# Work behind the value products done once per pair of tasks, one projection per slot

## The reference

```python
q, k, v = x @ wq + bq, x @ wk + bk, x @ wv + bv        # per head
x = layernorm(x + softmax(q k^T / sqrt(8)) v @ wo.T + bo)
# cross attention: per-head weights Wk, Wq, Wv (8 x 8); queries from x, keys and values from the context
x = layernorm(x + softmax((x Wq) (ctx Wk)^T / sqrt(8)) (ctx Wv) @ Wo.T)
# feed-forward 128 -> 512 -> 128, with activations and weights quantised to 8 bits over the whole tensor
x = layernorm(x + qlinear(gelu(qlinear(x, W1, b1)), W2, b2))
```

## Time and profile before

| | |
|---|---|
| median of 3 runs | 370.28 us (369.21 to 370.56) |
| profiled execution | 369.99 us, its span 368.3 us |
| attention stage | 25 to 285 us of the span |
| busy, whole span | DVE 329.0 us (89%), PE 269.9 (73%), ACT 254.9 (69%), POOL 189.1 (51%) |
| L771, maxima | 128 times, 155.7 us |
| L608 and L619, exponentials | 128 times, 131.2 us |
| TensorE's clock | 1.0 of full speed from 84 to 222 us |

### The profile page before, as it was taken

How to read it: one execution, slowest core, us unless ns; L and a number is a source line. 1 busy time by engine, 2 the same in 40 slices (tenths; PEclk the granted TensorE clock), 3 DMA queues, 4 the chain that set the end, 5 groups by cost and what they waited for, 6 DMA issues and landing times.

```text
span 368.3 us, 13210 instructions
## 1 busy us (share of the span) xinstructions
PE 269.9 (73%) x4899; PEld 172.1 (47%) x4899; DVE 329.0 (89%) x715; ACT 254.9 (69%) x501; POOL 189.1 (51%) x382
## 2 busy tenths in 40 slices
PE   3668778998898988989889898888882557102970
PEld 2445545565665655656556565555541312001640
DVE  5658798899999999999999999999989499998994
ACT  2136867787888877878788787777761499505965
POOL 5245778566656656566565566756122005400385
PEclk9999999899999999999999999999996565655796
DMA  1352332323323233232332323322000000000024
GB/s 50 100 152 68 85 88 61 97 74 105 96 76 104 83 89 103 70 105 69 103 104 70 110 73 105 91 83 76 10 5 1 0 0 0 0 0 3 0 87 142
DMA packets 48998, 25.19 MB, mean 68 GB/s; under 512 B 6440, under 2 KB 48808, under 8 KB 48936
## 3 DMA queue, kind: packets, MB, share of 16 engines
q1 hardware_dynamic: 48216, 24.02, 22.7%
q10 hardware_dynamic: 720, 0.33, 0.3%
HBM read 9.39 MB, written 2.10 MB: 31 GB/s over the span
## 4 chain that ended last, share of the span: by engine, by line
DVE 38%; PE 18%; issue 16%; POOL 10%; SPq 9%; ACT 4%; DMA 3%; DVEq 0%; POOLq 0%; ACTq 0%
DVE neg_max L771 14%; SPq L348 6%; DVE h_ext L880 5%; DVE h_ext L881 5%; PE ps L995 4%; PE ps L1021 4%; PE ps L1037 3%; POOL rstd L486 2%; DVE arena_q L905 2%; ACT probs L619 2%; POOL o_root L553 2%; DMA arena_h<-parts_cq 2%; DVE r_sum L781 2%; PE ps L1074 1%; PE ps L1063 1%
## 5 line engine op out<-in xcount | busy, mean ns | idle before, releaser
L771 DVE TENSOR_REDUCE neg_max<-ps 128x8 f32<-128x1024 f32 x128 | 155.7, 1216 | 12.4 <-PE ps L995 10.8
L608 ACT ACTIVATE probs<-ps 128x1024 f32<-128x1024 f32 x64 | 65.6, 1025 | 19.9 <-PE ps L1002 18.7
L995 PE MATMUL ps<-arena_h 31*128 31x128 f16 x1024 | 53.0, 222 | 34.7 <-DVE neg_max L771 22.7
L619 ACT ACTIVATE probs<-ps 128x1024 f32<-128x1024 f32 x64 | 65.6, 1025 | 17.2 <-PE ps L1002 15.8
L995 PEld LDWEIGHTS ps<-arena_h 31*128 31x128 f16 x1024 | 31.0, 95 | 67.5 <-DVE neg_max L771 41.9
L483 POOL TENSOR_TENSOR var_eps<-mean_var,eps_col 128x1 f32<-128x1 f32 x64 | 12.2, 191 | 82.0 <-DVE mean_var L818 82.0
L1002 PE MATMUL ps<-arena_h 32*128 32x128 f16 x1024 | 51.8, 219 | 0.5 <-ACT probs L608 0.5
L1021 PE MATMUL ps<-probs,arena_q 128*32 128x128 f32 x1024 | 42.2, 284 | 0.9 <-issue 0.9
L1021 PE MATMUL ps<-probs,arena_h 128*32 128x128 f32 x1024 | 41.2, 279 | 0.2 <-ACT probs L608 0.2
L486 POOL TENSOR_TENSOR rstd<-var_eps,minus_half 128x1 f32<-128x1 f32 x64 | 35.2, 550 | 5.2 <-PE ps L1021 0.2
L1002 PEld LDWEIGHTS ps<-arena_h 32*128 32x128 f16 x1024 | 29.6, 93 | 1.6 <-issue 0.9
(11 more groups left out here) (152 smaller groups left out, 642.5 us busy)
## 6 DMA issues: line engine op xcount, KB each, us to landing
arena_h<-parts_sq SPq DMA_DIRECT2D x48, 64.0 KB, 2.0
arena_h<-parts_ck SPq DMA_DIRECT2D x48, 64.0 KB, 2.0
arena_h<-parts_cq SPq DMA_DIRECT2D x48, 64.0 KB, 2.1
arena_h<-parts_sk SPq DMA_DIRECT2D x45, 64.0 KB, 2.0
xT_in<-in_xT_dram SPq DMA_DIRECT2D x16, 128.0 KB, 2.4
xN_in<-in_xN_dram SPq DMA_DIRECT2D x16, 128.0 KB, 2.3
cT_in<-in_cT_dram SPq DMA_DIRECT2D x16, 128.0 KB, 2.5
cN_in<-in_cN_dram SPq DMA_DIRECT2D x16, 128.0 KB, 2.5
```

The costliest lines, as they stand in the source:

```text
L608: act.activation(probs[1][:, :], ps_s2, ACT.Exp, scale=SCALE).then_inc(ex, 1)
L619: act.activation(probs[0][:, :], ps_s2, ACT.Exp, scale=SCALE).then_inc(ex, 1)
L771: dve.tensor_reduce(neg_max[b.par][:, HH * half:HH * half + HH], ps_s1.rearrange("p (h k) -> p h k", h=HH), AXX, ALU.max, negate=True).the ...
L995: ins = pe.matmul(ps_s1[:, at:at + S], q[r:r + MAX_AT, j, :], kk[r:r + MAX_AT, j, :], start=True, stop=True, skip_group_check=True)
```

## The change

Everything behind the value products is done once for both tasks of a pair. `whole(k)` gives the pair only when k is its second task. `ps_u` holds four quarters instead of two, `u_sb` 512 columns, `r_sum`, `att`, `attT` both tasks. ScalarE copies `u` and `cq_full` in even slots and `attT` in odd ones; VectorE has reciprocal, aggregates and `att` in the odd slot's first gap, both norms behind its second maximum, `y_sb` (one instruction for self pairs, two for cross pairs) in the even slot's first gap and both statistics in its second. GpSimd does `var_eps` and `rstd` on two columns, in odd slots. Only one projection stands in a slot: q six ahead, k five, v four, context key five, always behind the second burst; the copies of q and v are in the next slot. The first five pairs keep q and k in one slot. Loads of xT move one slot earlier.

```diff
-QK_AT, V_AT, CK_AT, FILL_AT, VC_AT, BIAS_AT = 5, 4, 5, 4, 3, -1
-XT_AT, XN_AT, CT_AT, CN_AT = 7, 3, 8, 6
+Q_AT, K_AT, V_AT, CK_AT, FILL_AT, VC_AT, BIAS_AT = 6, 5, 4, 5, 4, 3, -1
+XT_AT, XT_LEAD_AT, XN_AT, CT_AT, CN_AT = 8, 7, 3, 8, 6
-LEAD_SLOTS = 2
+def whole(k):
+    t = task(k)
+    return t if t is not None and t.half == 1 else None
...
# gpsimd
-                v = task(k - 4)
+                v = whole(k - 4)
                 if v is not None:
-                    pool.wait_ge(ag, v.pos + 1)
-                    pool.tensor_tensor(var_eps[v.par][:, :], mean_var[v.par][:, 1:2], eps_col[:, :], ALU.add).then_inc(ve, 1)
+                    pool.wait_ge(ag, 2 * v.at + 2)
+                    pool.tensor_tensor(var_eps[v.lane][:, :], mean_var[v.lane][:, :, 1],
+                                       eps_col[:, 0:1].broadcast_to([128, 2]), ALU.add).then_inc(ve, 1)
...
# scalar
+                zz, w, v = whole(k - 1), whole(k - 2), whole(k - 5)
...
+                if v is not None and v.kind == "S":
+                    act.wait_ge(tx, v.pair + 1)
+                    need(act, split_done["cq"], v.pair - RING + 1)
+                    act.copy(cq_full[v.ring][:, :], ps_x[:, 0:PAIR]).then_inc(txe, 1)
+                if zz is not None:
+                    act.wait_ge(pv, 2 * zz.pos + 2)
+                    need(act, tu, zz.at)
+                    act.copy(u_sb[:, :], ps_u).then_inc(ue, 1)
...
# vector
-                b, w, x, v = task(k + 2), task(k - 2), task(k - 3), task(k - 4)
+                b = task(k + 2)
+                w, x, v = whole(k - 2), whole(k - 3), whole(k - 4)
...
# tensor
+                w, x, v = whole(k - 2), whole(k - 3), whole(k - 5)
...
-                        need(pe, ue, z.pos)
+                        need(pe, ue, z.at)
...
-                if k >= LEAD_SLOTS:
-                    projections()
                 scores(1)
...
                 product(1)
...
+                projections()
```

More of the change, by code:

```diff
@@ L85, in __init__ @@
         self.par = pos % 2
+        self.at = pos // 2
+        self.lane = self.at % 2
     @property
@@ L187, in decoder_layer @@
         probs = [sb(f"probs{i}", [128, HH * S]) for i in range(HALVES)]
[L188 to L194, removed]
+        u_sb = sb("u_sb", [128, 4 * S])
+        r_sum, att, attT = sb("r_sum", [128, 2 * H]), sb("att", [128, 2 * H, E]), sb("attT", [128, PAIR])
+        y_sb = [sb(f"y_sb{i}", [128, 2, D]) for i in range(2)]
+        stats = sb("stats", [128, 2, 6])
+        mean_var = [sb(f"mean_var{i}", [128, 2, 2]) for i in range(2)]
+        var_eps = [sb(f"var_eps{i}", [128, 2]) for i in range(2)]
+        rstd = [sb(f"rstd{i}", [128, 2]) for i in range(2)]
         x2_all = sb("x2_all", [128, B, D])
@@ L638, in slot @@
                                        scale=w_inv[:, j:j + 1]).then_inc(w_magic, 1)
-                if v is not None and v.kind == "S":
-                    act.wait_ge(tx, v.m + 1)
-                    need(act, split_done["cq"], v.pair - RING + 1)
-                    act.copy(cq_full[v.ring][:, v.half * S:v.half * S + S], ps_x[:, 2 * S:3 * S]).then_inc(txe, 1)
             over_slots(slot)
@@ L788, in slot @@
[L788 to L794 removed]
+                    for i in range(2):
+                        dve.wait_ge(bs, 2 * v.at + i + 1)
+                        dve.bn_aggr(mean_var[v.lane][:, i, :], stats[:, i, :]).then_inc(ag, 1)
@@ L1082, in slot @@
-                if k < LEAD_SLOTS:
-                    projections()
+                if v is not None and v.kind == "S":
+                    pe.wait_ge(xn, v.pos + 1)
+                    need(pe, tae, pairs_to(k - 3))
+                    need(pe, mte, min(max(k + 2, 0), TASKS))
+                    for i in range(2):
+                        last = pe.transpose(ps_x[:, i * S:(i + 1) * S], x1_all[:, v.m - 1 + i, :], ident[:, :])
+                    last.then_inc(tx, 1)
+                product(1)
@@ new lines, in slot @@
+                if w is not None:
+                    pe.wait_ge(an, w.at + 1)
+                    need(pe, mte, min(max(k + 2, 0), TASKS))
+                    need(pe, tae, w.at)
+                    need(pe, txe, s_pairs_to(k - 6))
+                    for i in range(2):
+                        last = pe.transpose(ps_x[:, i * S:(i + 1) * S],
+                                            att[:, i * H:(i + 1) * H, :].rearrange("p h e -> p (h e)"), ident[:, :])
+                    last.then_inc(ta, 1)
```

298 lines of the change are left out of this document (159 added, 139 removed).

## The result

| | before | after |
|---|---|---|
| first set, median of 5 each | 370.31 us | 382.95 us, 1.036 of before (95% interval 1.032 to 1.039) |
| second set | 370.05 us | 385.16 us, 1.041 (1.035 to 1.047) |
| profiled execution, span | 368.3 us | 382.8 us |

The change costs 13 to 15 us. The forecast was 371.9, with 362.5 to 379 as its range: wrong in size, and the time lies beyond the range. In the changed kernel the maxima are L817, the bursts L1049 and L1056, the fills L376.

The account below looks back on a forecast made before the run. VectorE, all but full in the attention stage, was taken as the bound. Mixed stretch +2.2, cross-only +1.1, lead -2, end +0.6 and start 0 made +1.9 on 369.99: 371.9 us, range 362.5 to 379.

Parts of the forecast that it names:

- VectorE's work and the layout of the pair: Attention pair: net -0.2 us of VectorE work; even slot 3.45, odd 3.80 or 4.07, mean pair 7.49 us.
- TensorE: its bound: Projections behind the second burst take at most 0.45 us per slot; half slots hold 1.6 us of products or less.
- the floor of 1.72: Least time per half slot, maximum through burst to next maximum: 1.72 us, whatever VectorE does in between.
- ScalarE's copy of u behind `cq_full`: End of the even slot: this copy holds up the next product, 0.2 us in every second pair.
- The stack chain: Later rstd delays stack transfers; margin falls from 1.7 to 0.0 to 0.2 us, costing 0.3 us per pair.
- The max rows and the clock: Max row behind sq's issues lands near 8.5, needed at 8.8 us: covered, barely; no term for TensorE's clock.
- Cross-only: Stretch from 222 to 265 us: 7.37 us per pair plus 0.3 for late stacks, +1.1 us in all.
- The lead: Stretch from 41 to 84 us: one of two rstd behind memsets goes, -2 us, bounds -4 and +1.
- The start: ScalarE issues the first sk stack before copying v; SyncE's queue is behind anyway: 0 us.
- The second, slower by the stack chain: Late stacks set the pace: pairs of 8.1 us or more, 378 us in all (376 to 381), chance 0.24.
- Its condition: For the slower rival: GpSimd's split ends 5.2 us into the odd slot, against 4.9 forecast.
- its "against": Objection to the slower rival: a stall lengthens the pair and so gives the next stack its slack back.

Follow-up runs that it names:

- free_tight: `free` with u turned before the first value products, u copied before cq_full, and the maximum's wait written before the stack's: 366.82 us, 0.993 of before.
- free: Changed kernel with aggregates ending the even slot, cq split and sent first, max row before ck's transfers, first sk stack behind v's copy: 368.94 us.

## Why the prediction was wrong, point by point

The sum missed the span by 12.6 us: 5.5 in the mixed stretch, 3.0 in the cross-only one, 2.9 in the lead, 1.0 at the start, 0.2 at the end. The mechanism, stacks without slack, was the forecast's own. Five terms failed: the late max rows, the clock behind a stall, the stalls in the lead and the first stack's place at the start were put at nothing, and what stacks cost in the cross-only stretch at half.

- **VectorE's work and the layout of the pair: right.** 7.55 us per undisturbed pair against 7.49. The odd slot took 3.87 in one kind and 4.07 in the other (3.80 and 4.07 forecast), the second by the norms: 1.04 us for two where the other slots had 0.69. Those 1.04 end at 159.97, 0.09 us behind GpSimd's first instruction of the sq split (159.27 for 0.61). The Trainium skill's page SBUF — State Buffer, section SBUF: two separate sides, has the port pair as an exclusive lock; the trace agrees in these rows. With the aggregates moved, rstd comes earlier and the interval is 1.91 in both.
- **TensorE: its bound was wrong.** A projection was taken as 0.45 us at most behind the second burst; that of q takes 0.63 in the chain of `free_tight`, and with two transposes of a self pair the half slot is 2.00 us, above the floor of 1.72. The size came out nearly (0.27), since I had put 0.2 us there under another name, ScalarE's copy of u behind `cq_full`. That reason falls with `free_tight`.
- **The stack chain: right in time, somewhat low in price.** The split ends 5.0 us into the odd slot (4.9 forecast); the last issue starts 2.25 us before the burst could go for cross stacks, 2.64 for self (2.2 forecast, from 8.7 and 10.9). The price, (3.5 - 2.0 - 0.2) / 4 = 0.3 us per pair, takes one slow landing in four pairs. Ten of 18 were late, by 6.7 us: 0.37 per pair. All the last landings of the kernel before from 84 to 265 us could have been read: for cq 1.9 (five), 2.0, 2.1, 2.4, 2.8, 2.8, 3.0, 3.1, 3.2, 3.7, for sk 1.9 (five), 2.3, 2.5, 2.9, 4.0. Their mean excess over 2.2 is 0.40 and 0.32: 0.36. That it meets the 0.37 is in part luck: over the slack as it came out, 2.25 and 2.64, it is 0.37 and 0.18.
- **The max rows and the clock: put at nothing, the step that failed most in the mixed stretch.** "The max row, issued behind sq, lands near 8.5 and is needed at 8.8: covered, barely", and no term for TensorE's clock. Above the undisturbed 7.55 that stretch lost 9.6 us: 6.7 in the intervals in which the stacks were waited for and 2.9 in the others. Of these 1.2 are one clock dip, behind one of the ten late stacks; 1.6 are the four late max rows, none of them behind a stall. The miss of 5.5 us is 1.1 (7.55 for 7.49), 1.3 (0.37 for 0.3) and 2.9, with 0.2 of rounding.
- **Cross-only: the same, and a wrong undisturbed pair.** 7.82 and 7.32 us in turn, 7.57 in the mean where 7.37 was taken: 1.1 us; the rest of 46.9 above 5.75 x 7.57 = 43.5 is stalls and what follows them, 3.4 us where 1.7 stood. The slack was 2.05 us there.
- **A cause missed.** The lateness was put down to rstd alone. In cross pairs the copy of `ck_full` at the slot's end makes the split as late by itself. The forecast had its number ("only ready at 3.5") and used it for the norms, not for the chain. The two causes lie on top of each other, so the lateness came out; the experiments that undid one of them missed.
- **The lead: wrong in sign, 2.9 us.** -2 was taken since one of two rstd would go out of the memsets' way. It got +0.9: the sum had no stalls there, but the lead's pairs are held by the same stacks. Two intervals in front of cross pairs took 4.30 and 2.82 us, 2.4 and 0.7 too much, and the one behind the first, at the lower clock, 1.2. Without these 4.3 us the lead would have been 3.4 shorter than before, within the bounds of -4 and +1.
- **The start: wrong.** "SyncE's queue is behind anyway: 0". It is 1.0 us: ScalarE issues the first sk stack (three issues, 2.1 us) ahead of the copy of v, and the second pair's projection waits for that copy. With the old order the first maximum is at 14.6 again.
- **Rivals.** The second, slower by the stack chain, named the mechanism and the side, at 0.24. Its condition (a split that ends at 5.2) was not met; the scatter did it at 5.0. Its sign, pairs over 8 us, came: 8.08 in the mean of the mixed stretch. But that mean is of undisturbed pairs and of others up to 9.45, not of a chain that every pair pays. The stack behind each of the three longest stalls had 3.4 to 3.7 us of slack again, as its "against" said. With its price of 0.3 us more per pair, and the lead's gain still in it, it came to 378 us, 5 us under the time, for want of the same terms.

## What to carry to other kernels

When a change takes slack from a transfer, don't price the median landing and one outlier: take every landing of the old trace, set it against the new slack, and average the excess; here that gives 0.36 us per pair where 0.37 was measured, with some luck. Do it for every stretch, and for every other transfer of the same queue: "covered, barely" cost 1.6 us here, and 9 us in the versions that put more issues in front of the max rows. Follow each producer of a late step to the end, since two edits can hide behind each other, and undoing one then shows nothing. And where the pace is set by a loop of engines that wait for a transfer, a faster pair can give its gain back as stalls, as `free_tight` did with 4.4 of its 4.7 us.

## What the runs showed of the hardware

- The last of a stack's six transfers of 64 KB lands 1.9 us after the start of its issue at best, but takes over 2.5 us in 9 of 22 cases and up to 4.1 (8 of 23 and 4.0 in the kernel before). With loads of a sixteenth of the bytes it is just as often for cq (6 of 13).
- SyncE is busy 0.60 us (median) with issuing one of them, but up to 1.6 us in the changed kernel and 1.9 in the kernel before, and what stands behind it in the queue is late by as much.
- A VectorE norm that meets a running GpSimd instruction ends 0.08 to 0.10 us behind it: two norms took 0.59 us in `free` and 0.69, 1.04, 1.18 and 1.47 beside GpSimd's work.
- TensorE's granted clock fell to 0.5 (1.2 GHz) when a stall left it busy 0.20 of 2 us, and was back at 1.0 some 4 us later. It fell behind the stalls of 57 and 140 us, whose intervals were 4.30 and 3.38 us, but not behind those of 100 and 173 us (3.51 and 3.49), so the length alone does not decide.
- Waits in front of TensorE's first weight load: four semaphores, the maximum's written third, cost 0.24 us behind the maximum; the maximum's written first, the weight load starts 0.05 behind it. It was worth 0.19 us per even slot where TensorE was waited for, and nothing where VectorE was.
